# Second adapter products of a LoRA layer on two 64-row tiles of the array, for pairs of output tiles

## The reference

```python
# x: (128, 64, 1024)
A, Bw = lora_A_w[adapter_ids], lora_B_w[adapter_ids]      # rank 16, one adapter for each batch element
h = einsum('bsd,brd->bsr', x, A)
x = x + einsum('bsd,od->bso', x, base_weight) + base_bias + einsum('bsr,bor->bso', h, Bw)
# second layer: a long convolution along the 1024 positions, one filter K for each head (64 states)
y = irfft(rfft(x, 2 * L) * rfft(K, 2 * L))[..., :L] + x * D
x = x + y * (position < length)
```

## Time and profile before

| | us |
|---|---|
| median of 3 runs | 1149.46 |
| lowest, highest | 1146.32, 1150.1 |
| profiled execution | 1150.48 |
| its span, first to last instruction | 1148.8 |
| PE busy | 1128.8 (98%) |
| weight loads busy (beside the matmuls) | 976.9 (85%) |
| DVE busy | 720.2 (63%) |
| ACT busy | 530.6 (46%) |

### The profile page before, as it was taken

How to read it: one execution, slowest core, us unless ns; L and a number is a source line. 1 busy time by engine, 2 the same in 40 slices (tenths; PEclk the granted TensorE clock), 3 DMA queues, 4 the chain that set the end, 5 groups by cost and what they waited for, 6 DMA issues and landing times.

```text
span 1148.8 us, 15785 instructions
## 1 busy us (share of the span) xinstructions
PE 1128.8 (98%) x5824; PEld 976.9 (85%) x5824; DVE 720.2 (63%) x1108; ACT 530.6 (46%) x888; POOL 30.5 (3%) x78
## 2 busy tenths in 40 slices
PE   7899999999999999999999999999998999999998
PEld 6788888888888888888888888888887999999987
DVE  5766465546547465646557465635366888888886
ACT  4232160433142160433242160423267888888885
POOL 1000000000000000000000000000000000000000
PEclk9999999999999999999999999999998999999999
DMA  6695525354252525344251526335368989989883
GB/s 190 186 41 181 183 74 183 136 133 169 75 181 61 184 74 185 144 125 171 73 179 60 189 69 193 145 103 169 98 218 294 328 298 309 311 310 315 303 281 129
DMA packets 125442, 202.47 MB, mean 176 GB/s; under 512 B 17268, under 2 KB 99125, under 8 KB 121397
## 3 DMA queue, kind: packets, MB, share of 16 engines
q1 hardware_dynamic: 125364, 201.46, 56.2%
HBM read 117.41 MB, written 84.02 MB: 175 GB/s over the span
## 4 chain that ended last, share of the span: by engine, by line
PE 93%; DMA 3%; DVE 2%; SPq 1%; issue 1%; ACT 1%; DVEq 0%; ACTq 0%
PE acc L1204 58%; PE acc L1256 22%; PE acc L1216 5%; PE acc L1185 5%; PE acc L1279 2%; DMA out<-out_sb 1%; DMA x_scratch<-x_sb 1%; DMA w_raw<-w_t 0%; PE acc L1226 0%; DMA ids_sb<-ids 0%; SPq L341 0%; SPq L345 0%; DMA b_raw<-lora_b 0%; DVE x_sb L786 0%; SPq L350 0%
## 5 line engine op out<-in xcount | busy, mean ns | idle before, releaser
L1204 PE MATMUL acc<-x_hi,w_hi 128*128 128x512 f32 x1024 | 401.5, 392 | 11.2 <-DVE x_lo L741 8.0
L1204 PE MATMUL acc<-x_lo,w_hi 128*128 128x512 f32 x1024 | 399.6, 390 | 0.0
L1204 PE MATMUL acc<-x_hi,w_lo 128*128 128x512 f32 x1024 | 399.6, 390 | 0.0
L1204 PEld LDWEIGHTS acc<-x_hi,w_hi 128*128 128x128 f32 x1024 | 192.7, 188 | 48.1 <-issue 8.2
L1204 PEld LDWEIGHTS acc<-x_hi,w_lo 128*128 128x128 f32 x1024 | 192.7, 188 | 40.9
L1204 PEld LDWEIGHTS acc<-x_lo,w_hi 128*128 128x128 f32 x1024 | 193.0, 188 | 35.5
L786 DVE SCALAR_TENSOR_TENSOR x_sb<-acc,bias_sb,x_raw 128x512 f32<-128x512 f32 x128 | 94.2, 749 | 192.7 <-PE acc L1216 179.8
L1256 PE MATMUL acc<-u_hi,f_hi 128*128 128x512 f32 (+1 forms) x320 | 130.4, 407 | 0.0
L585 ACT ACT_TABLE_LOAD x16 | 20.5, 1283 | 235.1 <-DVE eg_f L902 235.1
L1256 PE MATMUL acc<-u_hi,f_lo 128*128 128x512 f32 (+1 forms) x320 | 120.2, 376 | 0.0
L1256 PE MATMUL acc<-u_lo,f_hi 128*128 128x512 f32 (+1 forms) x320 | 118.6, 371 | 0.0
(11 more groups left out here) (155 smaller groups left out, 1436.9 us busy)
## 6 DMA issues: line engine op xcount, KB each, us to landing
x_scratch<-x_sb SPq DMA_DIRECT2D x16, 2048.0 KB, 7.3
out<-out_sb SPq DMA_DIRECT2D x63, 512.0 KB, 5.5
x_raw<-x_t SPq DMA_DIRECT2D x15, 2048.0 KB, 12.3
u_raw<-x_scratch SPq DMA_DIRECT2D x14, 2048.0 KB, 13.3
wq_raw<-state_scratch SPq DMA_DIRECT2D x16, 1024.0 KB, 7.9
a_raw<-lora_a SPq DMA_DIRECT2D x128, 64.0 KB, 4.5
b_raw<-lora_b SPq DMA_DIRECT2D x128, 64.0 KB, 4.6
state_scratch<-g_sb SPq DMA_DIRECT2D x16, 512.0 KB, 3.1
```

Source lines behind the costliest of these rows:

```text
L1204: mm = pe.matmul(acc[:, n % O_BANKS, :], w, m, start=k == 0 and i == 0, stop=False)
```

## The change

`adapters_up` now takes a pair of output tiles, t and t + 1. The adapters' B of the even tile lies on rows 0 to 63 and that of the odd tile on rows 64 to 127, each as a high and a low part in buffers of their own; each matmul has 64 rows, so it is given a tile of the array of 64 x 128, at row 0 or row 64. For each half there are three partial products (high x high, high x low, low x high), each for the even and the odd tile in turn: 12 matmuls of 256 columns for a pair, where there were 8. The two tiles write different PSUM banks. The adapters' B is loaded with 16 DMAs of 32 KB for each group where there were 8 of 64 KB, and its halves are split with all 128 partitions.

The order on PE: in all groups the pair (t, t + 1) is added behind `base(g, t + 2)`, and the last pair behind `base(g, 7)`; `filters(c)` goes from t = 1 to t = 3. In group 0 weights tile 3 is split ahead of h, SP issues weights tiles 4 and 5 earlier, and DVE does `make_x1` of the first tiles between the splits of tiles 4 to 7. The steps of the filters are spread differently over a group. At the passage to stage 2, `states(0)` and `states(1)` both come first, in PSUM banks 0 and 1; `load_filters(1)` is issued ahead of the wait for the last x1, and `load_u(2)` behind the first output's store. Buffers are moved for this.

The diff, cut to its core:

```diff
@@ load_b (SP)
-                sp.dma_start(b_raw[j * rank:(j + 1) * rank, half, :, :].rearrange("p t n -> p (t n)"),
-                             lora_b[row, :, :].rearrange("a r n -> (a r) n")).then_inc(ld_b, 16)
+                for odd in range(2):
+                    first = odd * R2 + j * rank
+                    sp.dma_start(b_raw[first:first + rank, half, :, :].rearrange("p t n -> p (t n)"),
+                                 lora_b[row, odd * rank:(odd + 1) * rank, :].rearrange("a r n -> (a r) n"))\
+                      .then_inc(ld_b, 16)
...
             for i, row in enumerate(rows):
                 load_b(0, i, row)
-            for t in range(3, W_RAW):
+            for t in range(3, W_RAW + 1):
                 load_w(t)
             sp.dma_start(bias_sb[:, :], bias_t).then_inc(ld_bias, 16)
+            load_w(W_RAW + 1)
...
                     for q in range(EARLY // HQ):
                         load_u(q, 0, g)
+                    sp.wait_ge(m_h, n_groups)
+                    sp.wait_ge(c_alo, 2 * n_groups)
+                    load_filters(1)
                 sp.wait_ge(c_x1, NT * (g + 1))
-                if g == LAST:
-                    load_filters(1)
                 sp.dma_start(x1_d[g], x1_sb[:, :, :, :].rearrange("p h t b -> p (h t b)")).then_inc(st_x1, 16)
...
-            sp.wait_ge(m_o, NT * n_groups)
-            sp.wait_ge(st_x1, 16 * n_groups)
-            load_u(2)
             for h in range(heads - 1):
                 sp.wait_ge(c_y, h + 1)
                 sp.dma_start(out[h], out_sb[h % OUT_BUFS][:, :, :].rearrange("p t b -> p (t b)"))\
                   .then_inc(st_out[h % OUT_BUFS], 16)
+                if h == 0:
+                    sp.wait_ge(m_o, NT * n_groups)
+                    sp.wait_ge(st_x1, 16 * n_groups)
+                    load_u(2)
@@ ACT, group 0
             split_b(0)
+            split_w(3)
             split_h(0)
-            for t in range(3, NT):
+            for t in range(4, NT):
                 split_w(t)
@@ split_b (DVE; ACT's is alike)
-                minus_hi(b_st[R2:P, :, :, :], b_raw[:, :, :, :], b_st[0:R2, :, :, :]).then_inc(c_blo, 1)
+                minus_hi(b_st[:, 1, :, :, :], b_raw[:, :, :, :], b_st[:, 0, :, :, :]).then_inc(c_blo, 1)
@@ make_x1 (DVE)
-                dve.wait_ge(m_o, NT * g + t + 1)
+                dve.wait_ge(m_o, NT * g + t // 2 * 2 + 2)
@@ DVE, group 0
             split_b(0)
+            split_w(3)
             keep_own(0)
             split_h(0)
-            for t in range(3, NT):
-                split_w(t)
+            split_w(4)
             for g in range(n_groups):
                 make_x1(g, 0)
+                if g == 0:
+                    split_w(5)
+                    split_w(6)
                 make_x1(g, 1)
                 if g == 0:
+                    split_w(7)
                     filter_exponents()
@@ adapters_up (PE)
                 for half in range(2):
-                    for i, m in enumerate((hh, hl)):
-                        mm = pe.matmul(half_cols(acc[:, (NT * g + t) % O_BANKS, :], half), b_st[:, half, t, :],
-                                       half_cols(m[:, :], half),
-                                       start=False, stop=half == 1 and i == 1)
-                mm.then_inc(m_o, 1)
+                    for i, (part, m) in enumerate(((0, hh), (0, hl), (1, hh))):
+                        for odd in range(2):
+                            rows = slice(odd * R2, (odd + 1) * R2)
+                            last = half == 1 and i == 2
+                            mm = pe.matmul(half_cols(acc[:, (NT * g + t + odd) % O_BANKS, :], half),
+                                           b_st[rows, part, half, t // 2, :], half_cols(m[rows, :], half),
+                                           start=False, stop=last)
+                            if last:
+                                mm.then_inc(m_o, 1)
@@ PE, stage 1
             for g in range(n_groups):
-                lag = up_lag(g)
-                for t in range(lag):
-                    base(g, t)
-                adapters_down(g)
-                for t in range(lag, NT):
-                    if g == LAST and t == NT - 1:
-                        adapters_up(g, t - lag)
-                        base(g, t)
-                        continue
-                    base(g, t)
-                    adapters_up(g, t - lag)
+                base(g, 0)
+                if g == 0:
+                    base(g, 1)
+                adapters_down(g)
+                for t in range(2 if g == 0 else 1, NT):
+                    base(g, t)
+                    if t % 2 == 0:
+                        adapters_up(g, t - 2)
                     for c in range(n_chunks):
-                        if t == 1 and g == taps_group(c):
+                        if t == 3 and g == taps_group(c):
                             filters(c)
-                for t in range(NT - lag, NT):
-                    adapters_up(g, t)
+                adapters_up(g, NT - 2)
@@ PE, stage 2
             def taps_even(h):
+                if h < 2:
+                    pe.wait_ge(c_ulo, u_low_done(h))
...
+            states(0)
+            states(1)
             for h in range(heads - 1):
-                states(h)
+                if h >= 2:
+                    states(h)
                 taps_even(h)
```

More of the change, by code:

```diff
@@ L32, in lora_s4d_kernel @@
     L = NT * P
[L33 removed]
+    n_adapters = lora_b.shape[0]
+    rank = lora_b.shape[1] // 2
     batch = ids.shape[1]
@@ L158, in lora_s4d_kernel @@
     out_sb = [place(f"out_sb{i}", [P, NT, batch], F32) for i in range(OUT_EARLY)]
+    cursor[0] = a_raw_at
+    wq_raw.append(place("wq_raw1", [P, HQ, BLOCKS, P], F32))
+    assert cursor[0] <= b_raw_at
+    cursor[0] = b_raw_at
+    out_sb += [place(f"out_sb{i}", [P, NT, batch], F32) for i in range(OUT_EARLY, OUT_EARLY + 1)]
+    assert cursor[0] <= b_raw_end
     cursor[0] = x_raw_at + U_BYTES
-    wq_raw.append(place("wq_raw1", [P, HQ, BLOCKS, P], F32))
-    out_sb.append(place(f"out_sb{OUT_EARLY}", [P, NT, batch], F32))
+    out_sb += [place(f"out_sb{i}", [P, NT, batch], F32) for i in range(OUT_EARLY + 1, OUT_BUFS)]
     assert cursor[0] <= x_split_at
-    cursor[0] = x_split_at
-    u_raw.append(place("u_raw2", u_shape, F32))
-    out_sb += [place(f"out_sb{i}", [P, NT, batch], F32) for i in range(OUT_EARLY + 1, OUT_BUFS)]
+    u_raw.append(place("u_raw2", u_shape, F32, at=x_split_at))
     SET_TILES = 4
@@ L277, in u_source, with x1_source, x1_last, u_last @@
         return u_raw[h // HQ % U_BUFS][:, g0:g1, h % HQ, :, :].rearrange("p g t b -> p t g b")
[L279 to L284, removed]
+    def x1_source(h):
+        return x1_sb[:, h, :, :].unsqueeze(2)
+    PART_A, PART_B, ALL_TILES = slice(0, NT // 2 - 1), slice(NT // 2 - 1, NT // 2), slice(0, NT // 2)
+    def x1_last(h, part):
+        return x1_sb[:, h, :, :].rearrange("p (r i) b -> p r i b", r=2)[:, :, part, :]
+    def u_last(parts, h, part):
+        return parts[h % SETS][:, :, LAST * G:].rearrange("p (r i) b -> p r i b", r=2)[:, :, part, :]
     def half_cols(t, half):
@@ L292, in u_loaded, with v_done @@
         return 16 * (q // U_BUFS + 1)
+    def v_done(h, i):
+        if h < 2:
+            return 1 + h if i == 0 else (N_CHUNKS - 2) * (h + 1) + i
+        return (N_CHUNKS - 1) * h + i + 1
     def u_low_done(h):
@@ L459, in _ @@
             sp.dma_start(len_i[:, :], bass.AP(lengths.tensor, 0, [[0, P], [1, batch]])).then_inc(ld_len, 16)
-            for t in range(W_RAW, NT):
+            for t in range(W_RAW + 2, NT):
                 load_w(t)
@@ L586, in filter_e, with filter_step @@
                 sines(step, eg)
[L588 to L591, removed]
-                        continue
+            def filter_step(g, i):
+                c, kind = divmod(PER_GROUP * (g - 1) + i, UNITS)
+                if 0 <= c < n_chunks:
                     if kind == 0:
@@ L613, in _ @@
                     filter_pre()
-                if 1 <= g <= FILTERS_DONE:
-                    filter_steps(g)
+                for i in range(1, PER_GROUP):
+                    filter_step(g, i)
                 if g + 1 < n_groups:
@@ L999, in begin_unit, with filter_step, filter_taps @@
                     e_args(c, kind - 3)
[L1001 to L1010, removed]
-                        if g == taps_group(c):
-                            filter_evac(c)
+            def filter_step(g, i):
+                j = PER_GROUP * (g - 1) + i
+                if 1 <= j <= UNITS * n_chunks:
+                    finish_unit(*divmod(j - 1, UNITS))
+                if 0 <= j < UNITS * n_chunks:
+                    begin_unit(*divmod(j, UNITS))
+            def filter_taps(g):
+                for c in range(n_chunks):
+                    if g == taps_group(c):
+                        filter_evac(c)
             def filter_evac(c):
@@ L1080, in _ @@
                 for t in range(2, before):
```

(10 more changed lines are left out.)

66 lines of the change are left out of this document (34 added, 32 removed).

## The result

The changed kernel takes 1164.96 us in the median of 4 runs (1162.68 to 1165.91), against 1149.78 for the kernel before beside it: 1.0134 times as long (95% interval 1.0112 to 1.0156), 15 us slower. The profiled execution took 1164.81, its span is 1163.1. The busy time of the engines hardly tells it.

A forecast was written before the change was run, and what follows sets the result against it. PE, busy for 98% of the span, was taken to bound the kernel. The terms summed as 1150.48 + 9.6 + 0.2 + 0.2 - 8.2 = 1152.3, forecast as 1152 us, range 1145 to 1195.

The forecast's parts named there:

- The forecast's own case: Whole kernel: two lanes in parallel, passage as in the rows of `filters`, stage 2 wait gone; 1152 us, chance 0.48.
- rivals with other lanes (1171, 1190): Adapter pairs: lanes overlap only in part, 1171 us, chance 0.08; or weight loads one after the other, 1190, chance 0.25.
- The lanes: Adapter pairs: an even and an odd matmul stream side by side, 6 x 0.115 = 0.69 us a pair.
- The rival of loads one after the other (1190): Adapter pairs: weight loads in different rows can't overlap, a pair costs 1.70 us, +48 us; chance 0.25.
- The passage: Adapter pairs: going to 64-row tiles and back makes a pair 1.10 us against 0.95, +9.6 us for 64.
- The rival without cost of passage (1127): Adapter pairs: changing to 64-row tiles costs nothing, a pair takes 0.70 us, -16 us; chance 0.13.
- The other groups: Groups after group 0: 8 more DMA issues on SP, 3.6 us of 51.5, don't reach PE; 0.
- Group 0: Group 0: PE stands 4 us more ahead of the first adapter products, some 3.8 us of waits go; +0.2 us.
- The passage to stage 2: After the last pair: 2.1 us of `make_x1` and splits, covered by `states(0)` and `states(1)`; +0.2 us at most.
- The wait in stage 2: Stage 2: PE's 5.33 us wait and the low clock behind it go with earlier stores; -8.2 us.

The follow-up runs named there:

- e3: The changed kernel with the odd tile's matmuls on rows 0 to 63 too, 12 matmuls a pair in one lane: 1200.37 us.
- e4: The changed kernel with each pair's half 0 matmuls moved to the middle of a base product, so two passages a pair: 1186.74 us.
- e9: The changed kernel with B loaded by 8 DMAs of 64 KB a group instead of 16 of 32 KB: 1152.24 us.
- e1: The changed kernel with group 0's load of the exponents issued behind x1's first store and the load of x: 1157.11 us.
- e5: The kernel before with only load_u(2) and the waits for the last x1's store moved behind head 0's output: 1147.45 us against 1149.59.
- e6: The changed kernel with load_u(2) and its waits back ahead of head 0's output, load_filters(1) still early: 1164.15 us.
- e7: The changed kernel with load_filters(1) back behind the wait for the last x1, load_u(2) still behind head 0's output: 1169.72 us.
- e2: The changed kernel with the second adapter products as 8 matmuls of 128 rows a pair on the whole array: 1153.06 us.
- e8: The changed kernel with second adapter products on the whole array, B in 8 loads, and the exponents' load behind x1's first store: 1141.0 us.

## Why the prediction was wrong where it was

The forecast was 1152, a change that couldn't be told from none; it is 13 us more. The range (1145 to 1195) and the likeliest direction (slower, 0.57) held the result, but in part by luck. The forecast's own case went from 1145 to 1160, which 1165 is outside of; the range reached further up for rivals with other lanes (1171, 1190), which the runs rule out. Of the 0.57 for slower only 0.18 stood for the case that came true, and of the 13 us above the forecast 9 are a term that was put at 0. Step by step:

*The lanes.* Right: two 256-column matmuls in 0.117 us, weight loads in parallel. The Trainium skill (TensorE: Matmul & The Clock Gate, The mechanism) has matmuls of different row groups start some 4 ns apart; the records of a pair begin together (merged, "x2"), which agrees. The rival of loads one after the other (1190) is out: e3 shows what one lane costs.

*The passage.* The mechanism was right and the rows of `filters` the right ones to read: 0.09 and 0.11 going in, 0.09 and 0.11 coming out, as in the earlier trace rows. The Trainium skill's rule that a change of tiling mode drains TensorE (TensorEngine Tiling (Array Packing), Key Properties) agrees with these gaps; it names no price. The term was undersized: +0.15 a pair was forecast, +0.21 is measured, 13.5 us for 64 instead of 9.6. What was left out is the slower cadence of the base matmuls behind the pair, 0.06. The rows of `filters` had only about 0.02 of it; half of it comes from putting two tiles' adapter matmuls behind each other, which the base product behind the last two tiles of a group showed (5.48 instead of 5.45). A stretch next to the gap has to be measured start to start until the cadence is the old one again. The rival without cost of passage (1127) is out (e4: 0.41 for one more).

*The other groups.* This step failed. It said that eight more issues on SP, 3.6 us of 51.5, reach nobody, because A and B of the next group are due at its end. It asked when the moved DMAs themselves are due and not what stands behind them in the queue: a store whose landing SP waits for takes 27 us, and behind that wait stands x1's first store, which frees `x1_sb`. In the kernel before it landed at 91.1; `make_x1` needs 0.75 us behind it, so tile 0's bank was free only some 0.7 us before the base product that needs it (92.57). With 8 more issues in group 0's own loads and 8 in the next group's, the exponents' store began at 60.23 instead of 53.23 (51.83 in e9, which has 8 fewer in each). That took the margin away, and the cost was 9.1 us: 6.3 of wait, the rest low clock and restart. e1 and e9 show both links of it.

*Group 0.* Foreseen was PE standing some 4 us for h, in exchange for 3.8 us of other waits: +0.2, and 0.6 for its four pairs. Measured is a wait of 2.2 for `hl` and in sum 0 to group 1's first base product. Right in kind, 1 us off. A term is missing in the forecast, though: behind the wait for `hl` the clock is low as well (four base matmuls 0.427 us apart, granted clock 0.72 from 30 to 36 us; in e1 ten). What B's eight more issues cost in this stretch stands in e9: with 8 loads, group 1 begins 3.3 us earlier (62.21).

*The passage to stage 2.* +0.2 was forecast; the trace has 0.3 for `s_lo` and 0.2 for `s_raw`. Small, as forecast.

*The wait in stage 2.* -8.2 was forecast, -7.4 is measured for the stage with the 0.5 just named; the sum was right and its reason for the most part not, so this was luck. The step gave both moves, and thought of head 0's place ahead of `load_u(2)` as the main one. e5, e6 and e7 show that this place is worth 2 us alone and nothing beside the other move; the 1 MB of filters ahead of x1's store made this store 5 us longer, and with it everything that waited for it. e5 comes near the bound that the step had named (0 if head 1's store is then as late as head 0's was): the waits of 3.6 us stand at later heads.

With the measured terms: 1150.5 + 13.5 (pairs) + 9.1 (group 1) - 0.8 (group 0 without its pairs) - 7.4 (stage 2) = 1164.9.

What stays open: why some ten base matmuls behind a pair start 0.23 to 0.24 us apart instead of 0.227. It isn't a price of the change of tile alone: eight adapter matmuls on the whole array bring 0.03 to 0.04 of it too (e2, e8, and the end of a group before), four bring hardly any, and in e4 two returns bring little more than one. No run shows the cause.

## What to carry to other kernels

A tile of the array smaller than the whole one has to save more than its passage costs: here 0.41 us there and back against 0.24 saved, so two lanes lose though they overlap almost fully. Where two or more kinds of tile alternate, put as much work as possible behind one passage, and read its price from any line of the old kernel that already changes the tile, up to where the old cadence is back.

Before adding DMA issues to a queue, follow the queue to the next wait and past it, and look for the margin of what stands behind; a wait for a slow store belongs behind everything urgent. The slow store itself stays in the way even then (e1: the urgent one was issued 16.4 us sooner and landed 5.1 sooner). And when two moves aim at one wait, try each alone: here one of the two had all of the effect. A stop of PE costs more than its length: here 9.1 us for a wait of 6.3.

## What the runs showed of the hardware that was not expected

The store of the exponents, element by element (2 x 16 KB), takes 26 to 29 us from its issue to its landing (27.8 before, 27.1 here, 27.5 in e1, 26.2 in e9, 29.1 in e8), and a 2 MB store issued 10 us behind it took 21.4 us to land (e1) instead of 10.1. A 2 MB store lands in 6.3 us with nothing issued just ahead of it and in 11.5 us behind 1 MB issued 0.6 us earlier: over 80% longer for half as many bytes more. And PE's wait of 6.3 us cost another 2.5, because the first half of the base product behind it ran at the lower of the two clock levels (1.2 GHz: 12 matmuls 0.427 us apart, the granted clock 0.50 from 98.8 to 102 us).
